# Turning the per-step maxima: block transposition on VectorE and eight transfers, against one turn on TensorE and two transfers

## What is computed

```python
xn = _layernorm(x, axis=-1)
q = _apply_rope((xn @ wq).reshape(B, S, 16, 16)); k = _apply_rope((xn @ wk).reshape(B, S, 4, 16))
scores = einsum('bshd,bthd->bhst', q, k) / 4, masked causally
out = einsum('bhst,bthd->bshd', softmax(scores), v) @ wo
y = real(ifft(fft(xn) @ (w_re + i w_im))) + bias
return x + out + y
```

## Time and profile before

| | |
|---|---|
| median of 3 runs | 1093.08 us |
| the three runs | 1085.03, 1093.08, 1095.99 us |
| the profiled execution's own time | 1086.32 us |
| its span, first to last instruction | 1084.6 us |
| mean granted TensorE clock in it | 0.918 of full speed |
| PE busy | 1014.3 us (94%) |
| DVE busy | 736.6 us (68%) |
| ACT busy | 654.8 us (60%) |
| POOL busy | 324.3 us (30%) |
| DMA | mean 40 GB/s |

### The profile page before, as it was taken

How to read it: one execution, slowest core, us unless ns; L and a number is a source line. 1 busy time by engine, 2 the same in 40 slices (tenths; PEclk the granted TensorE clock), 3 DMA queues, 4 the chain that set the end, 5 groups by cost and what they waited for, 6 DMA issues and landing times.

```text
span 1084.6 us, 17598 instructions
## 1 busy us (share of the span) xinstructions
PE 1014.3 (94%) x6792; PEld 498.6 (46%) x6792; DVE 736.6 (68%) x887; ACT 654.8 (60%) x1305; POOL 324.3 (30%) x352
## 2 busy tenths in 40 slices
PE   8879899999999989999998999998999989999896
PEld 7645455444444434444535555444544434444224
DVE  6686767677688887688821576677688887788000
ACT  3324456646577746677775555654677746677662
POOL 6486751156470001470002283180110001100001
PEclk9856759999999979999998898996999989999779
DMA  5755070004410060010007017007000000000000
GB/s 155 145 141 64 30 108 11 21 15 99 83 41 2 2 88 11 30 47 5 3 3 97 11 51 117 12 30 108 12 11 2 1 1 11 11 2 1 1 1 20
DMA packets 35635, 43.46 MB, mean 40 GB/s; under 512 B 9312, under 2 KB 21216, under 8 KB 35552
## 3 DMA queue, kind: packets, MB, share of 16 engines
q1 hardware_dynamic: 35552, 42.35, 20.3%
HBM read 27.13 MB, written 14.68 MB: 39 GB/s over the span
## 4 chain that ended last, share of the span: by engine, by line
PE 79%; ACT 7%; DVE 6%; issue 5%; DMA 1%; POOL 1%; SPq 0%; POOLq 0%; ACTq 0%
PE psO L1256 26%; PE psA L1195 18%; PE psS L1242 18%; ACT prob_sb L912 5%; PE psS L1169 4%; DVE pmax L1032 3%; PE psS L1227 3%; PE psS L1229 2%; PE psA L1200 2%; DVE pmax L1030 2%; DMA q_st<-parts_scratch 1%; PE psS L1176 1%; PE psO L1271 1%; PE psA L1210 1%; ACT oraw_sb L921 1%
## 5 line engine op out<-in xcount | busy, mean ns | idle before, releaser
L912 ACT ACTIVATE prob_sb<-psS 128x512 f32<-128x512 f32 (+2 forms) x1152 | 579.7, 580 | 286.8 <-PE psS L1242 283.5
L1032 DVE TENSOR_REDUCE pmax<-psA 128x2 f32<-128x1024 f32 x384 | 458.4, 1219 | 118.7 <-PE psA L1195 117.7
L1242 PE MATMUL psS<-q_st,k_st 50*128 50x512 f32 (+3 forms) x1280 | 425.8, 447 | 12.8 <-ACT prob_sb L912 11.6
L1195 PE MATMUL psA<-k_st,q_st 48*128 48x512 f32 (+3 forms) x1280 | 371.9, 444 | 30.8 <-DVE pmax L1032 15.6
L1256 PE MATMUL psO<-prob_sb,v_sb 128*32 128x512 f32 (+3 forms) x2560 | 321.8, 577 | 13.3 <-ACT prob_sb L912 9.1
L1195 PEld LDWEIGHTS psA<-k_st,q_st 48*128 48x128 f32 x1280 | 180.9, 201 | 263.9 <-DVE pmax L1032 104.0
L1242 PEld LDWEIGHTS psS<-q_st,k_st 50*128 50x128 f32 x1280 | 208.8, 198 | 137.6 <-ACT prob_sb L912 120.3
L1030 DVE TENSOR_REDUCE pmax<-psA 128x4 f32<-128x512 f32 (+2 forms) x192 | 198.8, 1043 | 95.6 <-PE psA L1200 94.2
L798 POOL TENSOR_SCALAR_AFFINE_SELECT prob_sb<-prob_sb 128x512 f32<-128x512 f32 x128 | 81.0, 635 | 583.2 <-ACT prob_sb L912 583.0
L1256 PEld LDWEIGHTS psO<-prob_sb,v_sb 128*32 128x32 f32 x2560 | 52.0, 110 | 101.8 <-issue 43.6
L1200 PE MATMUL psA<-mask_r,mask_l 64*128 64x64 bf16 (+1 forms) x768 | 83.8, 219 | 0.0
(11 more groups left out here) (86 smaller groups left out, 507.8 us busy)
## 6 DMA issues: line engine op xcount, KB each, us to landing
q_st<-parts_scratch SPq DMA_DIRECT2D x42, 256.0 KB, 11.4
parts_scratch<-parts SPq DMA_DIRECT2D x64, 128.0 KB
k_st<-parts_scratch SPq DMA_DIRECT2D x48, 128.0 KB, 4.5
q_st<-spartT SPq DMA_DIRECT2D x256, 2.0 KB
out<-x_sb SPq DMA_DIRECT2D x16, 256.0 KB, 2.2
x_sb<-in_L_attn_x SPq DMA_DIRECT2D x7, 512.0 KB, 4.0
parts_scratch<-parts SPq DMA_DIRECT2D x32, 64.0 KB
oraw_sb<-in_L_attn_x SPq DMA_DIRECT2D x1, 2048.0 KB, 14.5
```

The costliest lines, as they stand in the source:

```text
L912: nc.scalar.activation(prob[:, g % DEEP, r0:r0 + hp, s0:CH], psS[:, bank % RING, 0:hp * w].rearrange("p (h s) -> p h s", h=hp), ACT.Exp).t ...
L1032: nc.vector.reduce_max(pmax[:, heads[0]:heads[0] + 3:2, i, q], psA[:, two:two + 2, :], AX.X).then_inc(S["a_free"], 1)
L1195: last = mm(bank[:, k * w:(k + 1) * w], q_st[lo:lo + ROWS, n % (2 * KV), heads[o * per + k] % 2, i * P:(i + 1) * P], k_st[lo:lo + ROWS, sl ...
L1242: last = mm(bank[:, h * w:(h + 1) * w], k_st[lo:lo + FULL, key_slot(n, tile), kv, tile % CT * P:(tile % CT + 1) * P], q_st[lo:lo + FULL, n ...
```

## The change

The block transposition on DVE goes. In its place TensorE turns the 32 columns of spart in one go: `turn_maxima` writes 32 rows of 128 values into a slot of psA, which stands in `SEQ_A` like a maxima use, and DVE copies them to spartT when it comes to that slot (`copy_shift`). spartT then has each maximum row along the queries, so that `load_shift` needs 2 transfers of 8 KB, in runs of 128 values. SP waits for the slot's a_free and no longer for spartT_ready.

The planner gets the job `m` (the turn): on PE 0.2 us as a whole-array operation, on DVE 0.3 us, and 2 in place of 8 issues for a shift. It takes the turn as soon as the maxima are ready and a slot is free; meanwhile it goes on with other work, but holds back further maxima uses once the turn is due. All four engine orders are therefore written anew.

```diff
-            count = {"shift": 8, "store": 4, "kload": 6, "qload": 6, "out": 1, "x": 1}[job[0]]
+            count = {"shift": 2, "store": 4, "kload": 6, "qload": 6, "out": 1, "x": 1}[job[0]]
...
             if use == LAST_OF[n]:
-                dve += 0.95
-                issue_dma(dve, ("shift", n))
+                dve += 0.7
+                turning.append((dve + 0.05, n))
...
+        def do_turn():
+            ready, n = turning.pop(0)
+            pe.append(("m", len(slots)))
+            end = full("full", 0.2, max(ready, slot_ready()))
+            seq_a.append(("m", n))
+            slots.append(on_dve(end, 0.3) + 0.1)
+            issue_dma(dve, ("shift", n))
...
-            if a_part == 0:
+
+            turn_at = max(turning[0][0], slot_ready()) if turning else big
+            if a_part == 1 and turning and (turning[0][0] <= now + 0.3 or next_a == len(A_USES) or A_USES[next_a] == LAST_OF[A_USES[next_a][1]]):
+                ready["a"] = big
+            if a_part == 1 and turn_at <= soon:
+                choice = "m"
+            elif a_part == 0:
...
-        spartT = sb("spartT", [P, 2, 2 * R * CT], fp32)
+        spartT = sb("spartT", [2 * R * CT, 2, P], fp32)
...
             def load_shift(n):
-                sp.wait_ge(S["spartT_ready"], n + 1)
+                sp.wait_ge(S["a_free"], turn_job(n) + 1)
                 for t in range(2):
-                    rows = q_st[t * HALF + ROWS:t * HALF + FULL, n % (2 * KV), :, :].bitcast(fp32)
-                    rows = rows.rearrange("o r (i k s) -> o (r i) k s", i=CT, k=CT)
-                    for k in range(CT):
-                        sp.dma_start(rows[:, :, k, :], spartT[32 * k + 16 * t:32 * k + 16 * (t + 1), n % 2, :]).then_inc(shift_in[n % 2], 16)
+                    rows = q_st[t * HALF + ROWS:t * HALF + FULL, n % (2 * KV), :, :].bitcast(fp32).rearrange("o r (i s) -> o (r i) s", i=CT)
+                    sp.dma_start(rows, spartT[t * R * CT:(t + 1) * R * CT, n % 2, :]).then_inc(shift_in[n % 2], 16)
...
-                nc.vector.transpose(spartT[:, n % 2, :], spart[:, :, :, :].bitcast(fp32).rearrange("p t k c -> p (t k c)")).then_inc(S["spartT_ready"], 1)
+                nc.vector.tensor_copy(spartT[:, n % 2, :], psA[0:2 * R * CT, 2 * (v % 2), 0:P]).then_inc(S["a_free"], 1)
...
+            def turn_maxima(v):
+                n = SEQ_A[v][1]
+                pe.wait_ge(S["spart_ready"], 2 * n + 2)
+                two = slot_free(v)
+                nc.tensor.transpose(psA[0:2 * R * CT, two, 0:P], spart[:, :, :, :].bitcast(fp32).rearrange("p t k c -> p (t k c)"), ident[:, :]).then_inc(S["a_full"], 1)
```

More of the change, by code:

```diff
@@ L117, in schedule @@
         on_at = {}
+        turning = []
         pooled = {}
@@ L441, in schedule @@
             else:
+                ready["m"] = turn_at
                 first = min(ready.values())
-                assert first < big, (ready, next_b, next_v, next_a, stage[:1], back[:1])
-                choice = min(("a", "b", "v"), key=lambda k: ready[k])
+                if first == big:
+                    now += 0.2
+                    continue
+                choice = min(("a", "b", "v", "m"), key=lambda k: ready[k])
                 if ready[choice] > first + 1.0 and (beside < BESIDE[step] or ready[choice] == big):
@@ L475, in attention_fourier_block @@
             waiting = []
-        elif job[0] != "a":
+        elif job[0] not in ("a", "m"):
             ACT_ORDER.append(job)
@@ L481, in attention_fourier_block, with turn_job @@
     ACT_ORDER += waiting
+    def turn_job(n):
+        return SEQ_A.index(("m", n))
     def back_job(e):
@@ L564, in attention_fourier_block @@
             "bank_full", "bank_free", "a_full", "a_free", "pv_done", "o_copied", "diag_masked",
-            "smax_ready", "spart_ready", "spartT_ready", "shift_in_0", "shift_in_1",
+            "smax_ready", "spart_ready", "shift_in_0", "shift_in_1",
             "rl_ready", "o_normed", "out_ready", "out_stored")}
@@ L1046, in shift, with copy_shift @@
                 nc.vector.tensor_tensor(spart[:, :, 1, :], halves, spart[:, :, 0, :].bitcast(fp32), ALU.subtract).then_inc(S["spart_ready"], 1)
[L1047 removed]
+            def copy_shift(n, v):
+                dve.wait_ge(S["a_full"], v + 1)
                 if n >= 2:
[L1049 to L1050 removed]
+                    dve.wait_ge(shift_in[n % 2], 32 * (n // 2))
+                nc.vector.tensor_copy(spartT[:, n % 2, :], psA[0:2 * R * CT, 2 * (v % 2), 0:P]).then_inc(S["a_free"], 1)
             def normalise_out(v):
@@ L1122, in _ @@
                     normalise_out(v)
+                elif SEQ_A[v][0] == "m":
+                    copy_shift(SEQ_A[v][1], v)
                 else:
@@ L1316, in _ @@
                     project_v(job[1])
+                elif job[0] == "m":
+                    turn_maxima(job[1])
                 elif job[0] == "e":
```

8 lines of the change are left out of this document (3 added, 5 removed).

## The result

The changed kernel took **1133.77 us** in the median of four executions (1126.71 to 1139.01), the kernel before 1089.05 on the same chip (1084.68 to 1095.99). The ratio is 1.040, with a 95% interval of 1.031 to 1.049: slower by 45 us. 1098 us had been predicted, with a range up to 1113.

The account below looks back on a forecast made before the run. PE was taken as the bound (94% busy), DVE in dry stretches, plus the clock. Terms 6.5 + 1.5 + 3.4 - 1.5 - 2.5 = +7.4, say +7 us, on the 1091.4 mean gave 1098 us; range 1079 to 1113.

Parts of the forecast that it names:

- The turn's size: Each TensorE turn was taken as about 0.27 us on PE, between bounds of 0.14 and 0.45 us.
- The copy behind three reductions at step 12: In step 12's dry stretch DVE's copy stands three reductions behind the parts; scores start some 8 us after smax, as before.
- SP's transfers are 64: Sign of being right: SP's transfers from spartT are 64, and SP's idle time grows.
- Amid step 14: Sign of being right: PE stays busy around 98% amid steps 13 to 15, each 0.3 to 0.5 us longer.
- The turn as a stall: Rival: in-order PE waits at turns for DVE's spart; 1113 us, deciding from about 4 us of open lateness; chance 0.2.
- the saving on the direct way: near 0: At dry boundaries such as step 12, six fewer SP issues are offset by the copy's place in DVE's order; near 0.
- on DVE, +1.5 us: Transposition replaced by copy; the turn's slot stalls the two-slot ring 0.3 us at five dry boundaries: +1.5 us (0.1 to 4).
- the new order, +3.4 us: Five further maxima uses in stretches without scores, each costing DVE's 0.67 us over PE: +3.4 us (0 to 4.7).
- the clock, -2.5 us: Step 24's shorter dry stretch may keep its clock, saving 5 us at even odds: -2.5 us (-5 to 0).
- the weakest step: The clock, said to move by more than all other terms, about 1 us for each 0.001 of its mean.
- Its own sign of being wrong: If the mean clock over the span leaves 0.91 to 0.93, it is the clock that decides.
- +6.5 us for the turns on PE: 24 of 32 turns cost PE 0.27 us each, eight cost nothing: +6.5 us (3.4 to 10.8).

Follow-up runs that it names:

- e1: Changed kernel's turns put into the old order of the kernel before, behind the first maxima use after a step's last: 1143.62 us, ratio 1.043.
- e5: Changed kernel with the shift transfers of steps 5, 12, 22 and 25 issued ahead of the chunk loads: 1111.93 us, ratio 1.021.
- e12: Kernel before, old order and DVE transposition kept, plus 32 idle slots (TensorE turn, DVE copy nobody reads) three maxima uses behind: 1123.69 us, ratio 1.032.
- e14: New order with the old DVE transposition and eight transfers, shifts of steps 5, 12, 22 and 25 ahead of the loads: 1121.99 us, ratio 1.032.
- e13: Kernel before plus TensorE alone turning 32 identity columns inside 31 existing maxima uses, without slot or copy: 1097.20 us, ratio 1.010.
- e4: Changed kernel with the transposition of each turn done twice into the same slot: 1127.60 us, ratio 1.040.
- e15: Changed kernel's turns in the old order of the kernel before, two further maxima uses behind each step's last: 1107.80 us, ratio 1.017.
- e16: Old order with the changed way, but 30 of 32 turns in free columns of existing maxima uses, without own slot: 1107.95 us, ratio 1.019.
- e7: Changed kernel's turns in the old order of the kernel before, three further maxima uses behind each step's last: 1120.02 us, ratio 1.030.
- the fills: First bank of most maxima uses in dry stretches computed twice: changed kernel 1137.72 us, kernel before 1099.53, old order with turns three uses behind 1125.42.
- e9: Changed kernel with the first bank computed twice in 62 maxima uses, in runs of four or more without scores between: 1137.72 us.

## Why the prediction was wrong, point by point

**Right.** The turn's size: 0.284 us in the median (0.27 taken), the copy 0.269 (0.28 worked out). The page of the Trainium skill that the prediction weighed (VectorE: DVE Perf Modes, section The three transpose paths) gives 390 ns, for 128x128 bf16, and the trace decides for less here; another of its pages (TensorE: Matmul & The Clock Gate, section PE-mode transpose) gives for the same shape some 275 ns in one kernel's context, and the median of 284 ns for the narrower turn here lies near it:

```profile
L1232 PE MATMUL psA<-ident,spart x32: 269/284/421, 60.8 to 1054.8; 128*32 128x128 f32 x32
...
L1072 DVE COPY spartT<-psA x32: 269/269/280, 61.5 to 1055.2; 32x128 f32<-32x128 f32 x32
```

The copy behind three reductions at step 12 came as drawn (3.95 us after smax), though the first scores of the step came 10.1 us after smax and not some 8. SP's transfers are 64. Amid step 14 TensorE is busy 39.25 of 40 us, and the step is 0.4 us longer (40.8 against 40.4 us between first scores). The turn as a stall was rightly left a rival for this order: 2.4 us of waits even by the weight loads, under the 4 us from which it was to decide. In the old order it does decide, as e1 showed.

**Wrong, the step that failed first: "the saving on the direct way: near 0".** The step reckoned the chain up to the end of the two issues, and took the time to landing from before. It counted what stands ahead of the copy on DVE, and not what stands ahead of the transfers on SP. There, loads had been put ahead of the shifts of five steps. From the end of the issues to the scores that wait for them it is 11.5, 10.2, 4.5 and 5.3 us at steps 2, 5, 12 and 25, not 2. The term was 0 and should have been about +20 (e5 against the changed kernel: 1.9% of 1087 us), 8.8 us of it as open waits.

**Too small: "on DVE, +1.5 us" for the slot.** The term was 0.3 us at five dry boundaries, with 4 as its upper end. At these five (steps 4, 8, 12, 24, 28) DVE stands idle behind the copy for 0.57, 0.87, 0.70, 0.22 and 0.70 us, 3.1 in all: twice the term, and within its bounds. What the bounds left out is that a slot can cost outside the dry stretches too, where TensorE runs ahead of DVE by two slots and now by one: 11.5 us more of waits in e12, in the old order.

**Too small: "the new order, +3.4 us".** It was reckoned as 0.67 us for each of five further uses. The dry stretches ahead of steps 8, 12 and 28 grew by 5.8, 5.2 and 4.1 us, 15 in all; 12 of them stand in e14 too, in which only the orders are new.

**Wrong in sign: "the clock, -2.5 us".** It was named the weakest step, with 1 us for each 0.001 of mean clock. The mean over all executions went from 0.918 to 0.897, 21 us by that rule and 27 by the table. The prediction reckoned the clock at the one dry stretch that gets shorter (step 24: gap 11.6 us for 14.8, as forecast), and not at those that get longer, nor at steps 5 and 25, where gaps of 7.3 and 5.3 us more came up that had hardly been there. Its own sign of being wrong, a mean clock outside 0.91 to 0.93, came true: "it is the clock that decides".

**The rest of the sum.** +6.5 us for the turns on PE is not contradicted (e13: 1.0%, interval 0.2 to 1.8%, though in its executions it shows as clock and not as work; e4 shows no rise). Beside the +20 for the shifts behind loads, the other 22 to 25 us of the changed kernel's loss are what e5 still has (2.1%), and they were not taken apart. Two things are of that size: the turn with slot, copy and later transfer, which costs 1.7 to 1.9% in the old order (e15, e16), and the new order by itself, which costs 3.2% in e14, 12.4 us of waits for its eight transfers included. In the new order the turns do not show as waits: those for the maxima are only 25.1 us (all rows, the turn's too) against 23.4. How the second half is shared between turn and order stays open.

**Open.** Why three uses behind costs 12 us more than two, though all is ready in both; e7 loses that and more by the clock alone (112 us against 94). What brings the clock down at one place and not at the next: the fills tell only that taking away a part of TensorE's idle time in the dry stretches does not keep it up. No version made here beats the kernel before.

## What to carry to other kernels

When a change re-plans an order, read the queue that issues the transfers as closely as the engines: a small transfer that an engine waits for must stand ahead of large loads in its queue, unless the loads themselves are urgent. A side job through a ring of two buffers can cost more than its own duration, since it takes one buffer of the producer's lead (11.5 us of waits for 32 idle slots here); what that comes to depends on the place, so try several before taking the trouble to keep the job out of the ring. And a price per event is to be taken over all places of the new order: what gets longer, not only what one hoped would get shorter.

## What the runs showed of the hardware

- Two transfers of 8 KB issued 3.5 us behind six of 256 KB on one queue reached their waiting reader 10.2 us after the last issue (11.5 us at another step); ahead of such loads their reader did not wait when it came 4.4 us after it.
- On a TensorE that is busy for 92% of the span, 32 more turns of 0.273 us (8.7 us) did not raise the median: 1127.6 us against 1133.8, within the scatter.
- The lower clock sets in at the same places of the order from one kernel to the next (ahead of step 12 for 14 us before, for 27 in the changed kernel and in e9), and a fill of 0.85 us in 14 did not move it. At other places it differs between executions of one order: at the end of the program it is low for 51 us in the changed kernel's profile, for some 20 in e4's. The Trainium skill (TensorE: Matmul & The Clock Gate, section A second HAM failure mode: psum-queue depth-cycling) tells of a kernel whose clock swings through short idle times between groups of matmuls as it cycles through its banks. The slots here are such a cycle, and e12 loses 25 us more to the clock than before; whether that is the mechanism no run here shows.
